# Routed experts in row tiles of 128: four experts' slots side by side as four column tiles, weights loaded four experts at a time

## The reference

```python
logits = x @ gate_weight.T; scores = softmax(logits)          # 64 experts in 8 groups
...                                                           # best 3 groups, then best 6 experts: topk_i, topk_w
flat = topk_i.reshape(-1)
pos = jnp.sum(jnp.cumsum(oh, axis=0) * oh, axis=-1) - 1        # place of a token in its expert
slot = flat * C + jnp.minimum(pos, C - 1)                      # C = 96 slots per expert
buf = zeros((E * C, H)).at[slot].set(x[tok]).reshape(E, C, H)  # E = 64, H = 256
g = jnp.einsum('ech,emh->ecm', buf, Wg)                        # M = 176
u = jnp.einsum('ech,emh->ecm', buf, Wu)
out = jnp.einsum('ecm,ehm->ech', silu(g) * u, Wd).reshape(E * C, H)
y = sum over the 6 choices of out[slot] * topk_w
```

## Time and profile before

| | |
|---|---|
| timed runs | 1814.08 us median (1811.03 to 1816.03) |
| profiled execution, its span | 1840.4 us |
| TensorE busy | 1555.0 us (84%) |
| VectorE busy | 1079.0 us (59%) |
| ScalarE busy | 761.4 us (41%) |
| GpSimd busy | 690.8 us (38%) |
| DMA | 142.55 MB, mean 77 GB/s |

### The profile page before, as it was taken

The page is one execution under the profiler, slowest core; times in us unless marked ns, Lnnn a source line. Parts: engine busy times, 40 slices in busy tenths (PEclk is TensorE's granted clock), DMA queues, the critical chain, the costliest instruction groups (busy, mean ns, idle before and its releaser), DMA issues. The chain is left out here.

```text
span 1840.4 us, 26235 instructions
## 1 busy us (share of the span) xinstructions
PE 1555.0 (84%) x7678; PEld 1023.0 (56%) x7678; DVE 1079.0 (59%) x2735; ACT 761.4 (41%) x1818; POOL 690.8 (38%) x677
## 2 busy tenths in 40 slices
PE   6889995548898978889993788689999999998798
PEld 3556654324455554555662566455666666665576
DVE  6842222376676547832224788477776766664788
ACT  5523332245555525533332111166655556553211
POOL 4553334454200003543335554055555545453000
PEclk9999997578999998999996888899999999999899
DMA  8319985122100005249972222000000000000000
GB/s 244 90 59 290 292 244 176 57 69 60 38 1 1 1 8 162 69 125 268 286 213 82 71 75 60 1 1 1 1 1 1 1 1 1 1 1 1 9 17 21
DMA packets 83395, 142.55 MB, mean 77 GB/s; under 512 B 15816, under 2 KB 43312, under 8 KB 83296
## 3 DMA queue, kind: packets, MB, share of 16 engines
q1 hardware_dynamic: 53600, 90.96, 17.0%
q0 software_dynamic: 15360, 37.77, 7.0%
q10 hardware_dynamic: 14336, 12.59, 2.5%
HBM read 122.39 MB, written 18.87 MB: 77 GB/s over the span
## 5 line engine op out<-in xcount | busy, mean ns | idle before, releaser
L2267 POOL TENSOR_TENSOR sb_m_prob<-sb_m_prob,sb_m_rinv 128x512 f32<-128x512 f32 x256 | 258.8, 1043 | 287.4 <-DVE sb_m_rinv L2316 287.4
L2223 ACT ACTIVATE sb_m_prob<-m_ps_s,sb_m_nmax 128x512 f32<-128x512 f32 x256 | 173.8, 683 | 204.1 <-DVE sb_m_nmax L2320 203.9
L1263 POOL DMA_INDIRECT sb_c_rows<-slot_rows,sb_slot x192 | 191.6, 998 | 130.7 <-DVEq L1284 57.9
L2320 DVE TENSOR_REDUCE sb_m_nmax<-m_ps_s 128x2 f32<-128x1024 f32 x128 | 156.4, 1222 | 127.8 <-PE m_ps_s L2118 127.8
L1097 POOL DMA_INDIRECT e_xn<-xn_rows,sb_table x128 | 118.0, 922 | 208.7 <-PE e_ps_x L1175 195.3
L1246 DVE TENSOR_TENSOR sb_e_h<-sb_e_sg,e_ps_gu 96x176 f32<-96x176 f32 x128 | 42.6, 333 | 255.2 <-ACT sb_e_sg L1222 208.7
L1184 PE MATMUL e_ps_gu<-e_wgu,sb_e_xT 128*96 128x352 f32 x512 | 177.2, 468 | 16.1 <-ACT sb_e_xT L1216 14.2
L2126 PE MATMUL m_ps_p<-sb_ident,sb_m_prob 128*128 128x128 f32 x1024 | 136.4, 273 | 15.8 <-ACT sb_m_pT L2231 11.3
L2126 PEld LDWEIGHTS m_ps_p<-sb_ident,sb_m_prob 128*128 128x128 f32 x1024 | 117.9, 141 | 41.2 <-POOL sb_m_prob L2267 13.8
L1201 PE MATMUL e_ps_y<-e_wdn,sb_e_hT 96*96 96x256 f32 x512 | 132.2, 382 | 0.0
L2117 PE MATMUL m_ps_s<-sb_m_latT_high,sb_m_qa 128*128 128x512 f32 x256 | 126.6, 495 | 1.1 <-ACT sb_m_prob L2223 1.1
(11 more groups left out here) (283 smaller groups left out, 3230.1 us busy)
## 6 DMA issues: line engine op xcount, KB each, us to landing
e_wgu<-wgu SPq DMA_DIRECT2D x128, 352.0 KB
e_wdn<-wdn SPq DMA_DIRECT2D x128, 192.0 KB
slot_rows<-sb_e_y ACTq DMA_DIRECT2D x128, 96.0 KB
xn_rows<-e_xn SPq DMA_DIRECT2D x16, 256.0 KB, 2.3
sb_c_rows<-slot_rows,sb_slot POOLq DMA_INDIRECT x192
sb_x<-x SPq DMA_DIRECT2D x4, 512.0 KB, 5.9
e_xn<-xn_rows,sb_table POOLq DMA_INDIRECT x128
sb_g_zm<-wqT SPq DMA_DIRECT2D x1, 2048.0 KB
```

The lines of the kernel that those rows point to most:

```text
L1263: pool.indirect_dma_start(rows[u][j][:, :], None, k.slot_rows[:, :], bass.IndirectOffsetOnAxis(ap=k.slot[:, n, j:j + 1], axis=0))\
L2223: act.activation(prob[s % 4][:, hh, :], ps_s[s % 2][:, hh, :], ACT.Exp, bias=nmax[s % 2][:, hh:hh + 1], accum_out=rsum[s % 2][:, hh:hh + 1 ...
L2267: pool.tensor_tensor(part, part, rinv[s % 2][:, hh:hh + 1].to_broadcast([P, T]), ALU.mult)\
L2320: dve.tensor_reduce(nmax[s % 2][:, :], ps_s[s % 2][:, :, :], AX, ALU.max, negate=True).then_inc(nmax_ready, 1)
```

## The change

One step is no longer an expert but a row tile: 128 rows, of which 32 belong to each of four experts (a quad). A quad has three such tiles (its slots 0 to 31, 32 to 63, 64 to 95), so there are 48 steps a round. Transposes are of 128 x 128. Gate/up and down are computed by four matmuls for each half of the contraction, one an expert, each with 32 columns of the stationary operand and its own 32 partitions of PSUM. The step loops are written out in full. Weights are laid out in DRAM by quads and loaded by quads into three buffers. There are eight gather buffers of 128 rows, all filled at the end of `route`, and four `y` buffers. The store of a tile goes to four separate blocks of 32 rows in `slot_rows`. The table is copied in 12 pieces of 32 partitions.

```diff
-AHEAD = 12
+GE = 4
+ROWS = P // GE
+THIRDS = CAP // ROWS
+QUADS = E0 // GE
+ROW_TILES = QUADS * THIRDS
+QB = 3
...
-            load_experts(0, AHEAD // 2)
+            load_quad(0)
             store(4)
             store(5)
-            load_experts(AHEAD // 2, AHEAD)
+            load_quad(1)
             store(6)
             store(7)
+            load_quad(2)
...
-            pool.wait_ge(table_ready, r + 1)
-            for e in range(XB):
-                gather_expert(pool, k, e, k.gathered[e])
+            for t in range(2 * XB):
+                if t < THIRDS:
+                    pool.wait_ge(table_ready, r * THIRDS * GE + (t + 1) * GE)
+                gather_rows(pool, k, t)
...
-            dve.tensor_copy(k.table[:, :], kept_table).then_inc(table_ready, 1)
+            for t in range(THIRDS):
+                for j in range(GE):
+                    dve.tensor_copy(k.table[j * ROWS:(j + 1) * ROWS, :].rearrange("p (a t) -> p t a", t=THIRDS)[:, t, :],
+                                    kept_table[t * ROWS:(t + 1) * ROWS, :].rearrange("p (a j) -> p j a", j=GE)[:, j, :])\
+                       .then_inc(table_ready, 1)
...
-    y_stored = [k.sem(f"e_y_stored{u}") for u in range(2)]
+    y_stored = [k.sem(f"e_y_stored{u}") for u in range(YB)]
...
+            for a in range(QB, QUADS):
+                q, left = a % QB, base + (a - QB + 1) * THIRDS
+                sp.wait_ge(gu_ready, left)
+                sp.dma_start(wgu[q][:, :, :, :], k.w["wgu0"][a]).then_inc(gu_got[q], 16)
+                sp.wait_ge(dn_ready, left)
+                sp.dma_start(wdn[q][:, :, :, :], k.w["wdn0"][a]).then_inc(dn_got[q], 16)
...
+                for c in range(DC):
+                    for j in range(GE):
+                        ins = pe.matmul(ps_gu[v][own(j), :], xT[v][:, c, own(j)], wgu[a % QB][:, j, c, :],
                                         start=(c == 0), stop=(c == DC - 1))
...
+            rows = k.slot_rows.rearrange("(a j t i) d -> a t j i d", j=GE, t=THIRDS, i=ROWS)
...
+                if g >= YB:
+                    act.wait_ge(y_stored[b], 16 * (g // YB))
+                act.activation(y[b][:, :], ps_y[v][:, :], ACT.Copy).then_inc(y_ready, 1)
+                act.wait_ge(y_ready, g + 1)
+                act.dma_start(rows[t // THIRDS, t % THIRDS], y[b][:, :]).then_inc(y_stored[b], 16)
...
-        k.table = k.sb("table", [CAP, E0], U32)
+        k.table = k.sb("table", [P, ROW_TILES], U32)
...
-        "wgu0": c(gu.reshape(E0, DC, P, 2 * M0).transpose(0, 2, 1, 3)),
-        "wdn0": c(down_chunks),
+        "wgu0": c(gu.reshape(QUADS, GE, DC, P, 2 * M0).transpose(0, 3, 1, 2, 4)),
+        "wdn0": c(down_chunks.reshape(QUADS, GE, MH, 2, D).transpose(0, 2, 1, 3, 4)),
```

More of the change, by code:

```diff
@@ new lines, in routed_experts @@
+        sg = [sb(f"e{r}_sg{u}", [P, M0]) for u in range(2)]
+        h = [sb(f"e{r}_h{u}", [P, M0]) for u in range(2)]
+        hT = [sb(f"e{r}_hT{u}", [MH, 2, P]) for u in range(2)]
+        y = [sb(f"e{r}_y{u}", [P, D]) for u in range(YB)]
+        ps_x = [ps(f"e{r}_ps_x{u}", [P, DC, P]) for u in range(2)]
+        ps_gu = [ps(f"e{r}_ps_gu{u}", [P, 2 * M0]) for u in range(2)]
+        ps_h = [ps(f"e{r}_ps_h{u}", [MH, 2, P]) for u in range(2)]
+        ps_y = [ps(f"e{r}_ps_y{u}", [P, D]) for u in range(2)]
@@ L1152, in _ @@
-            with sp.Fori(1, E0 // U) as i:
-                for u in range(U):
-                    load(i * U + u, u)
-            for e in range(E0 // U * U, E0):
-                load(e, e % U)
+            for a in range(QB, QUADS):
[4 more added lines that the diff above has]
+                sp.dma_start(wdn[q][:, :, :, :], k.w["wdn0"][a]).then_inc(dn_got[q], 16)
@@ new lines, in hidden_turned, with down @@
+            def hidden_turned(t):
+                v, g = t % 2, base + t
+                pe.wait_ge(h_ready, g + 1)
+                if g >= 2:
+                    pe.wait_ge(hT_ready, g - 1)
+                for c in range(2):
+                    ins = pe.transpose(ps_h[v][:, c, :], h[v][:, MHC[c]:MHC[c] + MH], k.ident[:, :])
+                ins.then_inc(hT_raw, 1)
+            def down(t):
+                a, v, g = t // THIRDS, t % 2, base + t
+                pe.wait_ge(hT_ready, g + 1)
+                if t % THIRDS == 0:
+                    pe.wait_ge(dn_got[a % QB], 16 * (quads_before(a % QB) + a // QB + 1))
+                if g >= 2:
+                    pe.wait_ge(y_ready, g - 1)
+                for c in range(2):
+                    for j in range(GE):
+                        ins = pe.matmul(ps_y[v][own(j), :], hT[v][:, c, own(j)], wdn[a % QB][:, j, c, :],
+                                        start=(c == 0), stop=(c == 1))
+                ins.then_inc(dn_ready, 1)
@@ L1233, in _, with tokens_copied @@
-            pipelined(act, step, U, last, U)
-            for v in range(2):
-                act.wait_ge(y_stored[v], 16 * ((r + 1) * E0 // 2))
+            rows = k.slot_rows.rearrange("(a j t i) d -> a t j i d", j=GE, t=THIRDS, i=ROWS)
+            def tokens_copied(t):
+                v, g = t % 2, base + t
+                act.wait_ge(xT_raw, g + 1)
+                if g >= 2:
+                    act.wait_ge(gu_ready, g - 1)
+                act.activation(xT[v][:, :, :], ps_x[v][:, :, :], ACT.Copy).then_inc(xT_ready, 1)
@@ L1237, in _ @@
+            for s in range(ROW_TILES + LAG):
+                if live(s):
+                    tokens_copied(s)
+                if live(s - 1):
+                    silu(s - 1)
+                if live(s - 3):
+                    stored(s - 3)
+            for b in range(YB):
+                act.wait_ge(y_stored[b], 16 * ((r + 1) * ROW_TILES // YB))
         @block.vector
         def _(dve):
-            def step(s, u, lap):
-                g = s + r * E0
-                if live(s, 1):
-                    v = (u - 1) % 2
-                    dve.wait_ge(act_ready, g)
-                    if later(s, 3):
-                        dve.wait_ge(hT_raw, g - 2)
-                    dve.tensor_tensor(h[v][:, :], sg[v][:, :], ps_gu[v][:, M0:2 * M0], ALU.mult).then_inc(h_ready, 1)
-                if live(s, 2):
-                    v = u % 2
-                    dve.wait_ge(hT_raw, g - 1)
-                    if later(s, 4):
-                        dve.wait_ge(dn_ready, g - 3)
-                    dve.tensor_copy(hT[v][:, :, :], ps_h[v][:, :, :]).then_inc(hT_ready, 1)
@@ L1257, in gather_tile @@
+            for s in range(ROW_TILES + LAG):
+                if live(s - 1):
+                    hidden(s - 1)
+                if live(s - 2):
+                    hidden_copied(s - 2)
 def gather_tile(pool, k, r, n, u, rows):
```

181 lines of the change are left out of this document (71 added, 110 removed).

## The result

The changed kernel takes 1853.24 us (median of four runs, 1843.64 to 1857.63) where the kernel before takes 1812.55 us (1807.21 to 1816.03) on the same chip: a ratio of 1.022, 95% interval 1.019 to 1.025. It is slower, as forecast, but by 40.7 us and not by 16.4.

What follows compares the result with a forecast made beforehand. It took TensorE, with DMA close behind, to bound the expert stage before, and four DMA engines after. Stage +5.1 and start +3.1 us made +8.2 a round, +16.4 in two: 1830 us, range 1775 to 1895.

Steps and rivals of the forecast that it cites:

- The sign and its mechanism: Routed experts: the new store runs on four engines (chance 0.88), whose work sets the period; slower overall (chance 0.55).
- The named wait: ScalarE's copy of ps_y into y waits for the store four tiles back, stopping the pipeline; 10 us of cover.
- Per round +8.2: Sum for one round of routed experts: stage +5.1 us and start 3.1 us later; two rounds +16.4 us.
- Mean 170.4 us: Routed experts in the kernel before: rounds of 168.6 and 172.2 us, the baseline for the stage.
- I carry the difference over: Whole kernel: timed runs 26 us below the profiled span, so a span of 1857 was turned into 1830 us.
- The next block begins 3.1 us later: End of route: eight gathers instead of four end at 128.2 us, delaying the expert stage by 3.1 us a round.
- The stage: Routed experts, one round: 7.5 us first quad, 13 x 12.0, then 12 at the end; 175.5 us, +5.1.
- A tile takes 2.5 us: TensorE in the expert stage: 2.5 us a row tile, 7.5 us a quad, where four experts take 9.5.
- Rival 1: Expert stage: four engines but less work, 10.7 us a quad, 162 us a round; 1796 us; 0.26 with all faster.
- Rival 2: Expert stage: all 16 engines take the store, 10.0 to 7.5 us a quad; 1778 to 1714 us; chance 0.10.
- Rival 3: Expert stage: four engines and a stalled pipeline, up to 15.8 us a quad, +58 us a round; 1929 us; chance 0.12.
- Rival 4: TensorE in the expert stage: column tiles run one after another, 408 us a round; near 2300 us; chance 0.02.

Runs made afterwards that it cites:

- e1: Changed kernel with each row tile stored whole to 128 consecutive rows instead of four blocks of 32 (rows land in wrong places): 1792 us, ratio 0.987.
- e2: Kernel before with each expert's 96 rows stored as four blocks of 24 rows lying apart: 1877 us, ratio 1.032.
- the second and third profile: Kernel before, unchanged, profiled twice more after the profile ahead of the prediction: 1805.45 and 1816.22 us.
- e8: Changed kernel with four gathers in route and the other four issued in the expert stage, instead of eight in route: 1837 us, ratio 1.013.
- e10: e9 with four gathers in route in place of eight: 1779.79 us, ratio 0.984.
- e16: Kernel before with its weights laid out in memory by quads, still loaded expert by expert: 1818 us, ratio 1.005.
- e17: Kernel before with four y tiles in the ring in place of two, nothing else: 1786.04 us, ratio 0.988.
- e9: Changed kernel with intermediate rows kept in tiles' order, so a tile's 128 rows are stored consecutively, output as the reference's: 1793.89 us, ratio 0.991.
- e11: e10 with the hidden layer turned ahead of gate/up, so two changes of tiling a step in place of four: 1787 us, ratio 0.988.
- e6: Changed kernel with eight y tiles in the ring in place of four: 1846 us, ratio 1.018.

## Why the prediction came out as it did

**The sign and its mechanism: right, and shown.** The four-block store runs on four engines (12672 packets in q10), and that alone makes the kernel slower: e1 and e2 show it from both sides, 61 and 64 us. The rule that the forecast weighed, in the Trainium skill, page DMA: Bandwidth & Descriptors, section Why a DMA increments its semaphore by 16 and not by 1, holds for a transfer with 128 on one side and 4 on the other; before the change only `be` spoke for it. The named wait (ScalarE's copy on the store four tiles back, everything behind it) is there, 24.6 us between 135 and 290. Beside it the forecast had nothing for the issue of a store, which holds ScalarE for another 18.6 us there.

**The size: off by 24 us of the median, and here the forecast failed.** The step that failed is the sum "Per round +8.2": it measures +16.4. Between profiles (changed 1841.9 us of span, before 1809.1 on the mean of the second and third profile) the difference is 32.9 us; the other 8 are scatter, the changed kernel's profiled run being its shortest. Against 16.4 forecast the 16.5 missing are these, for both rounds together:

- *The baseline, +6.1.* "Mean 170.4 us" came from an execution 26 us longer than the runs, and "I carry the difference over" put all of that outside the stage. 3 us a round were inside it.
- *The start, +3.9.* "The next block begins 3.1 us later": it is 5.05 (12.25 against 7.2 from the first gather). I let the block begin when the eighth gather ends; it begins 2.4 us after. In the kernel before the fourth gather ends 2.8 us before the block begins as well, and I had put that down to VectorE alone. e8 and e10 show the term: 16 and 14 us of the median with four gathers less.
- *The stage, +3.0*, 177.0 for 175.5 a round. That this term came out close is luck: two larger errors nearly cancel. In round 0 (177.5 us) the y stream has 10.5 us a quad on the mean; with 2.7 quads at TensorE's 9.1 us that leaves 10.7 for the 13 loaded ones, not 12.0, the low end of the range (16.5 us less). This is a mean and no steady period: single quads take 9.1 to 16.6 us. "A tile takes 2.5 us" missed the changes of tiling: a quad is 9.1 us, not 7.5. The quads without a load (24.3 us), the 8.9 us to the first store and the 4.8 behind the last make 38 us where 19.5 were summed (18.5 more). The drop of the clock had no term either; how much of the round it costs no run parts from the stalls.
- *Between the stages, +5.0*, a place that the forecast had at nothing. Every kernel with the change shows 486 to 489 us there, the kernel before, e16 and e17 481 to 484, e2 486. No experiment took it apart, but the traces place most of it: linear attention's first matmul waits for the load `sb_g_qp<-wo` and begins 22.2 us into its block in the changed kernel, 19.0 us in the kernel before. Why the load lands later stays open. The rest of the sum is -1.5.

**What bounds the kernel: the weak reading.** "DMA is saturated in two places" and "the stage is TensorE's, with DMA close behind" left 18 us a round unassigned. e17 shows 11 of them to be the ring of two, which neither engine's share tells. The trace had it: 29.2 us of waits for `y`, beside a rate that was below what two other stretches reach.

**Rivals.** Rival 1 had the right work a quad (10.7) and the wrong end, since it took TensorE's 7.5 us for granted. Rival 2 did not happen, but e9 prices it: 1794 us. Its range, 1714 to 1778, was too good; TensorE's step of 3.04 us ends it, and with a shorter step the stalls of e11. Rival 3's 15.8 us occur as single quads (up to 16.6 us in round 0), not as a mean. Rival 4 is out by the rows of one step.

**What the change is made of**, by these runs, in us of the median: ring of four -23 (e17); tiles, weights by quads and the rest -6 (e10 against e17, intervals overlapping: 0.980 to 0.987 and 0.986 to 0.991); eight gathers in `route` +14 (e9 against e10); store on four engines +59 (changed against e9). The sum is +44, measured +41. The tiling takes 6.5 us off a round (149.5 against 156.0 us), as TensorE's work does (64 x 2.38 = 152, 48 x 3.04 = 146). Of the 13 us, 6 are seen in the whole, since 487.0 us lie between the stages of e10 and 481.4 between those of e17.

## What to carry to other kernels

Before costing a change in a stage, price the stall that is already there: here a ring of two tiles more, an edit of a few lines, was worth 23 us, and the whole rebuild with everything mended 29 to 32. When a transfer's row blocks are rearranged, count how many engines will carry it (the endings of its queue, packets less rows, tell) and keep the outermost dimension of both sides one that 16 engines share, as 32, 96 and 128 were here and 4 and 8 were not, by relabelling the intermediate rows if need be. Read the records of the issues as well as the waits: a deeper ring only moved the hold from one to the other (e6). Take the baseline of a stage from a profile whose time is that of the timed runs.
